# Reordering the hand-written lists of the last stage: state-space block with feed-forward block on one Trainium2 core

## The reference, cut to what matters

```
h   = layernorm(x);  h_prev = h shifted by one token (zero at the start)
r   = sigmoid((mu_r*h + (1-mu_r)*h_prev) @ W_r.T)
k   = square(relu((mu_k*h + (1-mu_k)*h_prev) @ W_k.T))
out = x + layernorm(r * (k @ W_v.T))
```

## Time and profile before

| | |
|---|---|
| median of 3 runs | 256.66 us (256.44 to 256.72) |
| the profiled execution | 257.01 us |
| its span, first to last instruction | 255.2 us |
| PE, DVE, ACT, POOL busy, share of the span | 87%, 82%, 74%, 64% |
| mean granted TensorE clock | 0.974 |

### The profile page before, as it was taken

The page is one execution under the profiler, slowest core; times in us unless marked ns, Lnnn a source line. Parts: engine busy times, 40 slices in busy tenths (PEclk is TensorE's granted clock), DMA queues, the critical chain, the costliest instruction groups (busy, mean ns, idle before and its releaser), DMA issues.

```text
span 255.2 us, 6621 instructions
## 1 busy us (share of the span) xinstructions
PE 223.2 (87%) x1962; PEld 174.8 (68%) x1962; DVE 210.0 (82%) x646; ACT 188.1 (74%) x724; POOL 162.8 (64%) x279
## 2 busy tenths in 40 slices
PE   0895899688999998999999999999999999997930
PEld 0893444467788777868878886887688868755930
DVE  1779999987688987975998999889899987975762
ACT  2356748769987789876887797799769976977742
POOL 7433125666789698685868686867586775567351
PEclk9999689999999999999999999999999999999995
DMA  5980000000000000000000001000100100011023
GB/s 121 222 267 0 3 0 0 1 0 4 3 3 3 0 3 1 3 0 5 4 0 3 0 5 41 3 0 11 35 4 0 45 0 3 0 42 37 8 57 77
DMA packets 10199, 6.45 MB, mean 25 GB/s; under 512 B 864, under 2 KB 9856, under 8 KB 10160
## 3 DMA queue, kind: packets, MB, share of 16 engines
q1 hardware_dynamic: 10016, 5.77, 9.5%
q0 software_dynamic: 144, 0.21, 0.4%
HBM read 3.88 MB, written 2.10 MB: 23 GB/s over the span
## 4 chain that ended last, share of the span: by engine, by line
PE 48%; ACT 18%; issue 12%; DVE 11%; POOL 7%; DMA 2%; ACTq 1%; DVEq 0%; POOLq 0%
PE bank L979 9%; PE bank L1060 5%; PE bank L973 5%; PE pair L967 5%; PE bank L881 5%; ACT dt_all L747 4%; ACT bt L686 3%; PE bank L848 3%; PE bank L1120 2%; PE bank L1119 2%; ACT bank L675 2%; ACT junk L664 2%; PE bank L1096 2%; PE bank L1099 2%; DMA w_sb<-w_in 2%
## 5 line engine op out<-in xcount | busy, mean ns | idle before, releaser
L675 ACT ACTIVATE bank<-bank,rsn 128x512 f32<-128x512 f32 x32 | 21.1, 661 | 20.9 <-PE bank L881 20.8
L1377 DVE TENSOR_TENSOR x<-bank,wx 128x512 f32<-128x512 f32 x32 | 21.9, 684 | 16.6 <-ACT bank L675 13.6
L979 PE MATMUL bank<-x,sg 64*64 64x256 f32 x256 | 34.6, 385 | 0.0
L979 PE MATMUL bank<-xg,sg 64*64 64x256 f32 x256 | 33.8, 376 | 0.0
L967 PE MATMUL pair<-x,turned_bc 64*64 64x256 f32 x224 | 29.6, 376 | 0.0
L547 POOL TENSOR_TENSOR y<-ysum,zs 128x256 f32<-128x256 f32 x32 | 23.5, 734 | 6.3 <-DVE ysum L1400 6.2
L973 PE MATMUL bank<-st,bt 64*64 64x256 f32 x128 | 20.8, 395 | 5.9 <-ACT bt L686 5.0
L455 POOL TENSOR_TENSOR rb<-mse,halfn 128x2 f32<-128x2 f32 x32 | 23.5, 735 | 2.5
L452 POOL TENSOR_TENSOR mse<-msb,eps_all 128x2 f32<-128x2 f32 x32 | 8.0, 250 | 26.1 <-ACT junk L666 26.0
L979 PEld LDWEIGHTS bank<-xg,sg 64*64 64x64 f32 x256 | 21.4, 133 | 4.8
L427 POOL TENSOR_TENSOR x_lo<-xnT_all,x_hi 128x128 fp32r<-128x128 f32 x32 | 14.7, 460 | 14.8 <-ACT x_hi L590 14.8
(11 more groups left out here) (195 smaller groups left out, 763.4 us busy)
## 6 DMA issues: line engine op xcount, KB each, us to landing
x_all<-x SPq DMA_DIRECT2D x16, 128.0 KB, 4.3
out<-o_all SPq DMA_DIRECT2D x14, 128.0 KB, 2.5
cm<-consts SPq DMA_DIRECT2D x1, 640.0 KB, 5.4
w_sb<-w_in SPq DMA_DIRECT2D x1, 480.0 KB, 4.4
out<-o_all SPq DMA_DIRECT2D x4, 64.0 KB, 2.2
cm<-consts POOLq DMA_DIRECT2D x1, 128.0 KB, 4.2
wo_sb<-w_out SPq DMA_DIRECT2D x1, 128.0 KB, 4.8
bcb_sb<-bc_bias SPq DMA_DIRECT2D x1, 96.0 KB, 3.8
```

The costliest lines, as they stand in the source:

```text
L675: nc.scalar.activation(x_ps[:], x_ps[:], ACT.Silu, scale=rsn[:, par:par + 1]).then_inc(S["x_silu"], 1)
L979: mm = nc.tensor.matmul(y_ps[half(h)], sg[half(h), a, r], rx(x, r)[half(h)], start=start, stop=stop)
L1377: vec.tensor_tensor((x1, xg)[a][:, par].rearrange("p (a e) -> p a e", e=P), x_ps[:].rearrange("p (a e) -> p a e", e=P), wx[:, par, a].unsq ...
```

## The change

Only lists, waits and one bank number change. No instruction of PE or DVE is added or removed, and no tile's arithmetic changes. What is moved: the transposes of unit 6 go into bank 5 (free after the mask of the last tile), with the waits that follow from it; on POOL, `pool_outputs(4)` comes in one piece after `rstd(8)`; the outputs of unit 5 go from POOL to ACT, which does them after `gate_r(8)`; on DVE, `last_residual(4)` comes after `moments(7)`, `factor_terms(8)` ahead of `norm_biases(7)`, and `stats3(7)`, `moments(11)`, `gated_v(8)`, `stats3(8)` and `moments(12)` all come ahead of `norm_biases(10)` and `last_residual(6)`.

```
@@ ffn_bank @@
-            late = {5: (7, 7, 0, 1), 6: (7, 2, 0, 7), 7: (4, 5, 6, 3), 8: (4, 5, 6, 2)}
+            late = {5: (7, 7, 0, 1), 6: (5, 2, 0, 7), 7: (4, 5, 6, 3), 8: (4, 5, 6, 2)}
@@ POOL, last_ffn @@
                 factors(7)
-                pool_outputs(4, slice(0, 2))
                 rstd(7)
-                pool_outputs(4, slice(2, 4))
                 factors(8)
                 carry(7)
                 rstd(8)
-                rstd(9)
-                pool_outputs(5, slice(0, 4))
-                for k in range(10, len(rounds)):
+                pool_outputs(4, slice(0, 4))
+                for k in range(9, len(rounds)):
                     rstd(k)
@@ ACT, last_ffn @@
                 gate_r(8)
+                outputs(5)
                 outputs(6)
@@ PE, turn_normed @@
-                elif u == 6:
-                    pe.wait_ge(C["k_relu"], 6)
-                elif u == 7:
+                elif u < 8:
                     pe.wait_ge(S["sg_ready"], NT)
@@ PE, project_k @@
                 elif u == 7:
-                    pe.wait_ge(S["sg_ready"], NT)
+                    pe.wait_ge(C["shifted"], 7)
@@ PE, project_v @@
                 elif u == 6:
-                    pe.wait_ge(C["shifted"], 7)
+                    pe.wait_ge(C["k_relu"], 6)
@@ DVE, last_ffn @@
                 norm_biases(6)
-                last_residual(4)
                 residual(7)
                 stats2(7)
                 moments(7)
+                last_residual(4)
+                factor_terms(8)
                 norm_biases(7)
-                factor_terms(8)
                 residual(8)
@@
                 gated_v(7)
-                norm_biases(10)
-                last_residual(6)
                 stats3(7)
                 moments(11)
                 gated_v(8)
+                stats3(8)
+                moments(12)
+                norm_biases(10)
+                last_residual(6)
                 norm_biases(11)
                 last_residual(7)
-                stats3(8)
-                moments(12)
                 norm_biases(12)
                 last_residual(8)
```

## The result

The changed kernel takes 255.59 us (median of 17 runs, 254.89 to 256.45), against 256.48 us for the kernel before (17 runs). The ratio is 0.9963, with a 95% interval of 0.9951 to 0.9975: 0.95 us faster. The forecast was 255.4 us, that is 1.27 us faster, with a range of 254.7 to 256.1.

The account below looks back on a forecast made before the run. PE's list was taken as the bound up to unit 8's product, then SP's store issues. The last issue 1.27 us earlier gave 257.01 - 1.27 = 255.74 us profiled; the median lies 0.35 below: 255.4, range 254.7 to 256.1.

Parts of the forecast that it names:

- PE's earlier start: PE's turning of unit 6 waits for normed tiles, not the relu: starts 0.90 us earlier, and later products move with it.
- PE does not come earlier: Rival: another wait replaces the relu before PE's turning of unit 6; gain 0.4 us, time 256.3 us; chance 0.07.
- First half of the lists: DVE up to unit 4's residuals: at most 0.1 us won before moments 7; power for unit 8 0.37 us earlier.
- rival of a slow POOL: Rival: POOL's four outputs at up to 0.99 us hold round 9's power and DVE; gain 0.3 us, 256.3; chance 0.06.
- The rule that the prediction weighed: Round 7's power on POOL would hold DVE's unit 4 residuals, some 0.2 us worse; left out of the sum.
- Second half: DVE from unit 7's gates: 0.23 us slack before unit 8's gates, unit 6 later by 0.46, unit 8 written 3.2 earlier.
- SP, the next bound: SP's six last store issues can't follow the outputs that fast; the last issue moves only 1.27 us earlier, to 251.31.
- Leaving the loop: SP's cost between chunk 6's stores and those after the loop: between 0 and 0.80 us, taken as 0.2.
- one issue takes 0.63 us: Each store issue on SP was taken to cost 0.63 us, chunk 6's two going 0.84 us apart.
- The landing: Time for SP's last store to land at the end of the span: stays at 2.2 us, with 3.3 as slow bound.
- Stores not a bound: Rival: SP's issues much shorter than 0.62 us, so time follows DVE and ACT: 253.4 us; chance 0.03.
- slower through the stores: Rival: six gapless SP stores back up, landing after 3.3 us, leaving the loop costs 0.80: 257.1 us; chance 0.05.

Follow-up runs that it names:

- Bank only: The kernel before with only the other bank for the turning of unit 6 and its waits: 254.90 us, ratio 0.9960 to the kernel before.
- chunk 6 behind the loop: The changed kernel with chunk 6's pair of stores written out behind SP's loop instead of inside it: 254.83 us, ratio 0.9958 to the kernel before.

## Why the prediction was right, and where it was off

**PE's earlier start: right.** 0.90 forecast, 1.00 measured at the turning, 0.97 at the last product, with PE as busy in between as before. Bank only shows that this is the whole gain. The rival "PE does not come earlier" is out.

**First half of the lists: right that it costs and brings nothing.** The power of round 8 came 0.72 us earlier and not 0.37, since DVE was through with its factor terms 2.48 us after the last tile's product where I had counted 2.84. POOL's piece took 2.36 us for a forecast of 2.4, so round 9's power had 0.78 us to spare where I counted 0.28. The rival of a slow POOL is out. The rule that the prediction weighed, of the Trainium skill (SBUF — State Buffer, Who interferes with whom), that a DVE instruction with two SBUF inputs contends with a GpSimd one that reads SBUF, did not show beside the power: four residuals in 1.14 us, the same as the four of unit 5 at 239.48, when POOL was idle. If anything it was the power that gave way, by 0.05 us at most (0.74 us, where the later ones on two columns took 0.69 or 0.70). It did show, small, where POOL's outputs ran: the norm biases at 236.43 took 0.30 us in place of the usual 0.16. The trace was the better guide for a power on two columns.

**Second half: right.** DVE was idle 0.15 us before unit 8's gates (forecast 0.23), unit 6 came 0.44 us later (forecast 0.46). Unit 8 was written 2.92 us earlier (forecast 3.2), since ACT made eight outputs in a row and the last of them ended about 0.35 us later than the last residual alone would have allowed. (The recorded sum 245.69 + 1.14 + 0.6 + 0.6 gives 248.03 and not 248.05; nothing hangs on that.)

**SP, the next bound: the right mechanism, and the term that was mis-sized.** The first store of chunk 6 was issued at 17.61 us of the stage, for 17.63 in the forecast. Leaving the loop cost 0.21 us (249.27 less 249.06). The forecast had it at 0.2 without a row, so that this term fitted is luck. But the step "one issue takes 0.63 us" was wrong for the second store of chunk 6: 1.07. The three later ones kept their distances, so the last issue came 0.80 us earlier instead of 1.27. The landing was 0.15 us shorter, together 0.95.

**The forecast time is closer than the forecast gain, by luck.** 255.4 us is 1.27 below 256.66, the median of the three early runs of the kernel before. Over 17 runs that median is 256.48; the same gain would then have given 255.2, and the measured 255.59 is 0.4 from that and not 0.2. The gain itself was 0.95 us, three quarters of what was forecast.

**Stores not a bound, and slower through the stores:** both out. Four issues for unit 8 made it slower, ACT's issues faster, and no last landing of SP in these profiles was over 2.8 us.

**What the lists are worth.** I costed them with the bank, and the sum hid what the experiments took apart: with SP's stores as they are, lists alone win nothing and the bank alone wins everything. So much of the prediction's working, on DVE, POOL and unit 8, is right about steps that did not move this kernel's time. The new order at the end trades unit 6 against unit 8, and a train of six issues starts when unit 6 is written.

## To carry to other kernels

When a change brings the last results closer together, count the issues of the queue that stores them: from the first result that starts the train, each issue costs its 0.6 to 0.7 us, here for 32, 64 and 128 KB alike. Every unit is stored in two halves; no run stored both halves with one issue, so what half as many issues would give is open. An engine that has nothing left to do (here ACT, behind its last output) can issue the last stores at once. And take a reordering apart before it is kept: here one bank number and three waits did what a rewriting of three lists was credited with.

## What the runs showed of the hardware

In the last stage a store issue on SP took 0.60 to 0.64 us in nearly all cases, but in each profile of a kernel with an edit one or two issues of the last stage took 0.83 to 1.69. The trace's DMA records show a fetch of 16 KB of instructions beside every one of these. In the changed kernel the fetch runs from 247.49 to 248.66 us, and the issue begun at 247.99 ends at 249.06. The stretch from 247.4 to 248.7 us in the view of DMA queues (packets, MB, share of 16 engines):

```profile
q1 hardware_dynamic: 120, 0.06, 18.1%
q8 instruction: 1, 0.02, 5.6%
```

There are 15 such issues in the 13 profiles, and each ends 0.39 to 0.41 us after the end of its fetch, whether it took 0.83 or 1.69. (Two more issues took 0.67 and 0.73, in the second profile of the changed kernel and with chunk 6 behind the loop, each with a fetch of 8 KB beside it.) In the kernel before, a fetch of 16 KB runs from 248.38 to 249.61, and the two issues nearest to it took 0.62 and 0.64, so the earlier trace rows gave no hint. A fetch alone is not enough, though: the changed kernel's issue at 244.62 lies beside one that ends at 245.06 and took 0.62. What more is needed, which engine's code is fetched, and whether the fetch holds the issue or both follow something else, stays open; no run moved the fetch by itself. The first of ACT's two issues took 0.75 to 0.77 us in the four kernels that had them, also where SP had nothing to issue beside it.
